# Graph convolution as (adjacency · features) · weight, SAGE weight sums moved into the feed-forward stage, and another order of sums in the SAGE layers

## The reference, cut to what matters

```
x = x + relu(diffusion(h))                                   # 3 hops over a symmetric adjacency
x = x + layernorm(x1 + gelu(x1 @ W_ffn1 + b) @ W_ffn2 + b2)  # x1: relational layer, 4 edge types
x = x + D^-1/2 (A + I) D^-1/2 @ (h @ weight) + bias          # graph convolution (GCN)
x = x + sage(relu(sage(h)))                                  # two SAGE layers:
#   sage(x) = mean over in-edges of x @ Wl.T + bl + x @ Wr.T
```

## Time and profile before

| what | us |
|---|---|
| median of three runs | 365.51 (364.59 to 366.06) |
| the profiled execution, its own time | 366.03 |
| span of that execution in the trace | 364.1 |
| PE busy | 346.9 (95%) |
| DVE, POOL, ACT busy | 245.3, 135.1, 83.8 |

### The profile page before, as it was taken

One profiled execution on the slowest core, in us unless ns is written; L12 is line 12 of the kernel. 1 busy time (PEld: TensorE's weight loads), 2 busy tenths in 40 slices (PEclk: granted clock), 3 DMA queues, 4 the chain that ended last, 5 costly groups with the idle time before them and its releaser, 6 DMA issues.

```text
span 364.1 us, 4411 instructions
## 1 busy us (share of the span) xinstructions
PE 346.9 (95%) x1633; PEld 243.7 (67%) x1633; DVE 245.3 (67%) x407; ACT 83.8 (23%) x183; POOL 135.1 (37%) x102
## 2 busy tenths in 40 slices
PE   8999999998999999999999999999998957999996
PEld 3459898773488888888888888444556423474444
DVE  5899999998798788913865220176896685354543
ACT  3556663314200000000010421213133401112110
POOL 5000000008799999997020200000880084522020
PEclk9999999999999999999999999999999896999999
DMA  7100005089100000512000986600510000000003
GB/s 249 40 2 3 2 2 225 8 198 367 70 0 2 1 0 2 189 43 72 17 2 4 275 201 107 108 0 0 90 28 1 1 0 0 2 2 0 0 0 117
DMA packets 43831, 22.08 MB, mean 61 GB/s; under 512 B 35552, under 2 KB 36064, under 8 KB 43808
## 3 DMA queue, kind: packets, MB, share of 16 engines
q1 hardware_dynamic: 43280, 20.85, 21.1%
q0 software_dynamic: 240, 0.79, 0.7%
q10 hardware_dynamic: 288, 0.13, 0.1%
HBM read 20.72 MB, written 1.05 MB: 60 GB/s over the span
## 4 chain that ended last, share of the span: by engine, by line
PE 79%; DVE 15%; ACT 2%; issue 2%; DMA 1%; ACTq 0%; DVEq 0%
PE bank L1463 14%; PE bank L1577 13%; PE bank L1520 13%; PE bank L1688 13%; PE bank L1643 6%; PE bank L604 4%; PE bank L1726 4%; PE bank L577 4%; PE bank L601 3%; PE bank L1451 2%; DVE h L1167 2%; PE bank L593 2%; DVE stats L1115 2%; DVE lo L1185 1%; DVE x L1131 1%
## 5 line engine op out<-in xcount | busy, mean ns | idle before, releaser
L995 ACT ACTIVATE columns<-mean_var,eps 128x1 f32<-128x1 f32 x20 | 5.9, 294 | 132.8 <-DVE mean_var L1116 132.8
L890 POOL TENSOR_TENSOR spare<-slots 128x512 f32<-128x512 f32 x4 | 6.0, 1491 | 76.0 <-PE bank L1463 75.3
L1577 PE MATMUL bank<-slots,wall 128*128 128x256 f32 x128 | 30.2, 380 | 0.0
L1463 PE MATMUL bank<-slots,h_t 128*128 128x512 f32 x64 | 28.7, 594 | 0.8 <-ACT h_t L1006 0.8
L1463 PE MATMUL bank<-h_t,spare 128*128 128x256 f32 x128 | 28.1, 379 | 0.0
L1643 PE MATMUL bank<-slots 128*128 128x512 f32 x64 | 27.8, 592 | 0.0
L604 PE MATMUL bank<-slots 128*128 128x112 bf16 x256 | 27.8, 228 | 0.0
L1688 PE MATMUL bank<-wall,h_t 128*128 128x512 f32 x48 | 24.1, 634 | 2.7 <-ACT h_t L1006 1.8
L1577 PEld LDWEIGHTS bank<-slots,wall 128*128 128x128 f32 x128 | 24.2, 190 | 3.2
L1463 PEld LDWEIGHTS bank<-h_t,spare 128*128 128x128 f32 x128 | 24.2, 190 | 3.2
L601 PE MATMUL bank<-slots 128*128 128x140 bf16 x128 | 26.2, 242 | 0.0
(11 more groups left out here) (248 smaller groups left out, 734.7 us busy)
## 6 DMA issues: line engine op xcount, KB each, us to landing
slots<-in_L_gnn_W_rel SPq DMA_DIRECT2D x4, 1024.0 KB, 10.7
spare<-in_L_gnn_W_ffn SPq DMA_DIRECT2D x1, 2048.0 KB, 8.0
slots<-in_L_gnn_W_ffn SPq DMA_DIRECT2D x1, 2048.0 KB, 8.6
slots<-in_L_gnn_Wl SPq DMA_DIRECT2D x32, 64.0 KB, 2.4
slots<-in_L_gnn_Wr SPq DMA_DIRECT2D x32, 64.0 KB, 2.5
x<-in_x SPq DMA_DIRECT2D x4, 256.0 KB, 5.9
bias<-in_L_gnn_W SPq DMA_DIRECT2D x2, 512.0 KB, 5.6
slots<-in_L_gnn_W_self SPq DMA_DIRECT2D x1, 1024.0 KB, 5.6
```

Source lines behind the costliest of these rows:

```text
L1463: ins = pe.matmul(bank, left, right, start=start and i == 0, stop=stop and i == len(pairs) - 1)
L1577: ins = pe.matmul(into, left[:, k, tile(p)], right[:, k, :], start=(n in (0, 2, 3, 5) and r == 0 and k == 0), stop=False, skip_group_check ...
```

## The change

- GCN: instead of `A · (h · weight)` the kernel computes `(A · scaled h) · weight`. ScalarE writes `hi = relu(...)` directly with the degree's root folded into the scale (`root_by_degree`), DVE makes the same value in fp32 (`h`) and the rest `lo`. `near(k, q, ...)` multiplies them by the adjacency with the features as output rows, so that its result, copied out of PSUM by ACT and DVE in turns, is already the left operand of the product with `w2`. The four fills of `h` for the GCN go.
- Adjacency: ACT thresholds the transposed counts with two RELUs (`adjacency`), POOL adds the identity.
- Loads and sums of the SAGE weights: SP starts `load_turned` 0, 1, 2, 3 in a row and then `w2`; DVE does all sixteen `turn` ahead of the down stage; POOL does `combine_own(0)` and `combine_own(1)` ahead of the four additions of `bf2`.
- SAGE: DVE does `sum_nodes(layer, 1)` behind P4's addition instead of ahead of P5's, `sum_nodes(0, 0)` earlier; PE makes the fills 0 and 1 of layer 0 inside the product with `w2`, and the fill of tile 2 stands behind P1.

```diff
-        w2 = place(0)
-        sage_raw = [place(1), place(2), place(3), place(4)]
+        w2 = spare[:, KT * N:2 * KT * N].rearrange("p (k n) -> p k n", k=KT)
+        sage_raw = [place(1), place(2), place(3), place(0)]
...
             load_turned(0, wl1_in)
-            sp.dma_start(w2, tiled(w2_in)).then_inc(w2_loaded, 16)
             load_turned(1, wr1_in)
             load_turned(2, wl2_in)
-            sp.wait_ge(down_ready, NT)
             load_turned(3, wr2_in)
+            sp.wait_ge(up_ready, GT)
+            sp.dma_start(w2, tiled(w2_in)).then_inc(w2_loaded, 16)
...
-            for t in FFN_TILES:
-                pool.wait_ge(t_ready, use_of(H_FFN, t) + 1)
-                pool.tensor_tensor(h[:, t, :], h[:, t, :], bf2, ALU.add).then_inc(ffn_biased, 1)
-            pool.wait_ge(late_rows_loaded, 16 * 3)
...
-            pool.wait_ge(down_ready, NT)
-            combine_own(0)
+            for layer in range(2):
+                combine_own(layer)
+            for t in FFN_TILES:
+                pool.wait_ge(t_ready, use_of(H_FFN, t) + 1)
+                pool.tensor_tensor(h[:, t, :], h[:, t, :], bf2, ALU.add).then_inc(ffn_biased, 1)
+            pool.wait_ge(late_rows_loaded, 16 * 3)
+
             for t in range(NT):
-                pool.wait_ge(h_ready[TO_GCN], t + 1)
+                own = adj[:, t, t * P:(t + 1) * P]
+                pool.wait_ge(steps_out, 2 * t + 2)
+                pool.tensor_tensor(own, own.bitcast(F32), ident[:], ALU.add).then_inc(adj_ready, 1)
+            for t in range(NT):
+                pool.wait_ge(gcn_lo, t + 1)
                 pool.tensor_tensor(x[:, t, :], x[:, t, :], b2, ALU.add).then_inc(gcn_biased, 1)
-            base(0, 0)
-            combine_own(1)
-            base(0, 1)
+            for p in range(2):
+                base(0, p)
...
+            def adjacency(t):
+
+                act.wait_ge(cnt_t_ready, t + 1)
+                act.activation(both_ways[:, t % 2, :], (misc_bank if t % 2 else cnt_bank)[:], ACT.Relu, bias=ones[:, 0:1], scale=-1.0)\
+                    .then_inc(steps_out, 1)
+                act.wait_ge(steps_out, 2 * t + 1)
+                act.activation(adj[:, t, :], both_ways[:, t % 2, :], ACT.Relu, bias=ones[:, 0:1], scale=-1.0).then_inc(steps_out, 1)
+
             for t in range(NT):
                 root(OUT_FFN, t)
-                root(TO_GCN, t)
-                norm_relu(TO_GCN, t)
+                if t == NT - 1:
+                    adjacency(3)
+                root_by_degree(t)
+                act.wait_ge(shift_ready[TO_GCN], t + 1)
+                act.activation(hi[1][:, t, :], x[:, t, :], ACT.Relu, bias=shift[:, t:t + 1], scale=rstd[:, t:t + 1])\
+                    .then_inc(gcn_hi, 1)
+                if t < NT - 1:
+                    adjacency(t)
...
-            for k in range(KT):
-                turn(0, k)
+            for q in range(4):
+                for k in range(KT):
+                    turn(q, k)
 
             for m in range(NT):
                 dve.wait_ge(down_ready, m + 1)
...
                 scale_and_shift(TO_GCN, m)
-                if m == 2:
-                    for k in range(KT):
-                        turn(1, k)
+                dve.wait_ge(shift_ready[TO_GCN], m + 1)
+                link(dve.tensor_scalar(h[:, m, :], x[:, m, :], rstd[:, m:m + 1], shift[:, m:m + 1], ALU.mult, ALU.add))
+                dve.wait_ge(gcn_hi, m + 1)
+                dve.scalar_tensor_tensor(lo[1][:, m, :], h[:, m, :], 0.0, hi[1][:, m, :].bitcast(F32), ALU.max, ALU.subtract)\
+                    .then_inc(gcn_lo, 1)
...
+                    dve.wait_ge(sage_ready[layer], made(p, P5))
+                    dve.wait_ge(based, 2 * done)
+                    dve.tensor_tensor(own[:, 2 * p + 1, :], p53[:], own[:, 2 * p + 1, :], ALU.add).then_inc(own_sum, 1)
+                    dve.wait_ge(sage_ready[layer], made(p, P4))
+                    dve.tensor_tensor(out_of_lower, p74[:], upper, ALU.add).then_inc(lower_out, 1)
                     if p == 0:
                         sum_nodes(layer, 1)
...
+            transpose_counts(range(2, NT))
+            for q in range(NT):
+                pe.wait_ge(adj_ready, NT + q + 1)
+                if q < NT - 1:
+                    pe.wait_ge(gcn_lo, q + 1)
+                    for k in range(KT):
+                        if q == 0:
+                            pe.wait_ge(down_out, k + 1)
+                        near(k, q, (hi, lo))
+                else:
+                    pe.wait_ge(gcn_hi, NT)
+                    for k in range(KT):
+                        near(k, q, (hi,))
+                    pe.wait_ge(gcn_lo, NT)
+                    for k in range(KT):
+                        near(k, q, (lo,))
             pe.wait_ge(w2_loaded, 16)
             for m in range(NT):
...
+                    if (m, k) in ((2, 2), (3, 2)):
+                        fill_h(H_SAGE1, m - 2, h_ready[TO_SAGE])
+                    ins = pe.matmul(gcn_bank[m][:], h_t[:, k, tile(m)], w2[:, k, :], start=(k == 0), stop=(k == KT - 1))
+                ins.then_inc(gcn_ready, 1)
```

More of the change, by code:

```diff
@@ L677, in build_matrices @@
     return tails, block_out
-H_REL, H_FFN, H_GCN, H_SAGE1, H_SAGE2 = range(5)
+H_REL, H_FFN, H_SAGE1, H_SAGE2 = range(4)
 FFN_TILES = [2, 0, 3, 1]
-FILLS = [(what, t) for what in (H_REL, H_FFN, H_GCN, H_SAGE1, H_SAGE2) for t in (FFN_TILES if what == H_FFN else range(NT))]
+FILLS = [(what, t) for what in (H_REL, H_FFN, H_SAGE1, H_SAGE2) for t in (FFN_TILES if what == H_FFN else range(NT))]
 B = 32
@@ L777, in run_blocks @@
         dw_inv = sb("dw_inv", [P, HOPS, NT], F32)
-        columns = sb("columns", [P, 8, NT], F32)
-        std, rstd, shift, row_sum, inv_row, out_deg, deg_root, inv_root = (columns[:, i, :] for i in range(8))
+        columns = sb("columns", [P, 9, NT], F32)
+        std, rstd, shift, row_sum, inv_row, out_deg, deg_root, inv_root, eps_deg = (columns[:, i, :] for i in range(9))
         in_degs, inv_degs = sb("in_degs", [P, 2 * NT], F32), sb("inv_degs", [P, 2 * NT], F32)
@@ L995, in root, with root_by_degree @@
                 act.activation(std[:, t:t + 1], mean_var[:, t, 1:2], ACT.Sqrt, bias=eps[:]).then_inc(std_ready[n], 1)
+            def root_by_degree(t):
+                act.wait_ge(var_ready[TO_GCN], t + 1)
+                act.activation(std[:, t:t + 1], mean_var[:, t, 1:2], ACT.Sqrt, bias=eps_deg[:, t:t + 1], scale=out_deg[:, t:t + 1])\
+                    .then_inc(std_ready[TO_GCN], 1)
             def norm_relu(n, t):
@@ L1408, in _ @@
                 own = (h, x)[layer]
-                sum_nodes(layer, 0)
+                if layer == 1:
+                    sum_nodes(layer, 0)
                 for p in range(2):
@@ L1418, in _ @@
                     dve.wait_ge(first_kept, done)
-                    dve.tensor_tensor(upper, p6[:], first, ALU.add).then_inc(upper_sum, 1)
+                    dve.tensor_tensor(upper, p6[:], first, ALU.add).then_inc(sage_sum, 1)
                     if p == 1:
@@ L1647, in _, with near @@
-            transpose_counts(range(2))
+            def near(k, q, parts):
+                ins = product(main[k][:], [(part[1][:, q, tile(k)], adj[:, q, :]) for part in parts],
+                              start=(q == 0 and hi in parts), stop=(q == NT - 1 and lo in parts))
+                if q == NT - 1 and lo in parts:
+                    ins.then_inc(near_ready, 1)
+            transpose_counts(range(2, NT))
[14 more added lines that the diff above has]
+                        near(k, q, (lo,))
@@ L1696, in sage_products @@
                 for n in SAGE_ORDER[p]:
+                    if (layer, p) == (0, 0) and n in (P6, P7, P5):
+                        pe.wait_ge(gcn_out, 2 + (P6, P7, P5).index(n))
                     if n == P2:
@@ L1723, in mean @@
                         pe.wait_ge(out_lo, NT * layer + q + 1)
-                    for part in (hi[1 - layer], lo[1 - layer]):
+                    for part in (hi[layer], lo[layer]):
                         left, right = (cnt_r, part[:, q, :]) if exact else (wall[:, R], part[:, q, :].bitcast(F32))
-                        ins = pe.matmul(main[m][:], left[:, q, tile(m)], right, start=(q == 0 and part is hi[1 - layer]),
-                                        stop=(q == NT - 1 and part is lo[1 - layer]))
+                        ins = pe.matmul(main[m][:], left[:, q, tile(m)], right, start=(q == 0 and part is hi[layer]),
+                                        stop=(q == NT - 1 and part is lo[layer]))
                 ins.then_inc(mean_ready[layer], 1)
```

175 lines of the change are left out of this document (68 added, 107 removed).

## The result

| | median us | range | beside it: before |
|---|---|---|---|
| changed kernel, 4 runs | 374.59 | 374.13 to 376.56 | 365.78 (364.59 to 366.73) |

The ratio is 1.0248, with a 95% interval of [1.0205, 1.0291]: 8.8 us slower, where the prediction had 373.0 us and 90% for slower.

What follows compares the result with a forecast made beforehand. PE was taken to bound the kernel, busy 346.9 of 364.1 us. SAGE, 11.7 us shorter at 69.9, would start at 301.7 behind the delayed queues: span 371.6, 373.0 us in terms of the runs, range 369.5 to 379.5.

Steps and rivals of the forecast that it cites:

- 2: weight 3 turned: DVE's queue: four turns take 2.49 us after the last load lands at 240.5, so weight 3 is turned at 243.0.
- no hole at P3: PE in SAGE layer 0: the hole of 6.67 us goes, 6.84 us off.
- Step 1: SP's queue: loads 1 to 3 take 8.5 us each, are issued by 238.6, and the last lands at 240.5.
- Step 3: POOL's queue: combine_own(1) starts at 243.0, takes 9.9 us and is over at 252.9.
- Step 4: Down stage: DVE's first addition waits for two bf2 additions of 1.26 us each, starting at 255.5 instead of 234.4.
- only one queue counts: Down stage, rival: bf2 additions not held behind the combinations, DVE starts 12.5 us earlier, time 360.5; chance 6% for faster.
- The chain of the four tiles: DVE and ACT behind the down product: four tiles in sequence, 7.2 us each, 28.8 in all.
- Contention on tile 3: DVE's last chain beside POOL's GCN bias additions: between 0 and 2.5 us, middle 1.3 taken.
- The clock: PE at half clock after idling, around the product with w2: 0.5 us added, bounds 0 and 1.8.
- SAGE: From the first SAGE product to the end: 11.7 us off 81.64, so 69.9 us.
- first half-clock term: PE at the first SAGE product, 282.46: half clock behind the hole goes, 3.57 - 1.72 = 1.85 us off.

Runs made afterwards that it cites:

- Experiment 1: The changed kernel with POOL's additions of bf2 moved ahead of both combinations of SAGE weights: 366.01 us, ratio to before 1.0014.
- Experiment 6: The changed kernel with POOL's four additions of the GCN bias all behind the last lo: 373.32 us, ratio to before 1.0246.
- experiments 3, 4 and 5: The kernel before with combine_own(1) behind base(0, 1), 357.74 us; with sum_nodes(layer, 1) behind the additions for P5 and P4, 358.81 us; with both edits, 356.31 us.

## Why the prediction was right

Its numbers beside those of the changed kernel, 2.3 taken off for the late start:

| step | predicted | measured | off |
|---|---|---|---|
| 1: last load issued | 238.6 | 240.1 | +1.5 |
| 2: weight 3 turned | 243.0 | 244.3 | +1.3 |
| 3: `combine_own(1)` done | 252.9 | 253.8 | +0.9 |
| 4: first down addition | 255.5 | 256.3 | +0.8 |
| last `lo` ready | 285.6 | 286.4 | +0.8 |
| product with `w2` starts | 286.6 | 287.8 | +1.2 |
| first SAGE product | 301.7 | 302.5 | +0.8 |
| end of the span | 371.6 | 372.4 | +0.8 |

What was to show it, shows: the first addition released by L973, and 43.5 us of idleness on DVE up to it, broken only by turns; 18.0 us of idle PE, where more than 10 were foretold; no hole at P3; SAGE 70 us long. Point by point:

- **Step 1 was mis-sized by 1.5 us**, the largest error. With `w2` out of the way load 1 still took 9.80 us, between the 8.5 taken and the 12.00 of before; so about 2.2 of the excess were `w2`'s doing and 1.3 were not. The other traces agree: this load took 9.18 to 9.88 us in the five experiments with `w2` behind the loads, 11.64 to 12.40 in the three with `w2` in front of it. What the 1.3 are was not tried.
- **Step 3 came out 0.4 shorter**, which took back part of that: four instructions of 2.34 to 2.35 us. The shortest of the earlier trace rows were the right price for POOL alone.
- **Step 4 held, and so did its cause.** Experiment 1 removed just this wait and took 8.6 us off. The rival "only one queue counts" had this as its way to faster, with a price of 12.5 us: the wait was indeed 12.05 long, but 3.9 came back as contention, so even with it the kernel would not have been faster. That price had left the contention out.
- **The chain of the four tiles** took 7.18 us a tile for 7.2.
- **Contention on tile 3** was 1.3, the middle that was taken. Both operations were held, the fp32 copy of `h` (0.55 to 1.23) as well as `lo` (0.69 to 1.67), though neither for a whole POOL instruction. Here the rule of the Trainium skill that the prediction weighed ("SBUF — State Buffer", "Who interferes with whom") told what the first rows couldn't: that a tensor_scalar of 128x512 loses time too. It is not true of every tensor_scalar: one of 128x1 at 285.54, beside the same additions, took its usual 0.21 us. Experiment 6 gives the 1.3 back on DVE, though not at the end of the kernel.
- **The clock** cost 0 of the 0.5 taken. The windows of the changed kernel (length, busy us of PE, PEld, DVE, ACT, POOL with their counts; then the granted clock, DMA share, GB/s) show half clock from 264 on:

```profile
264.00:272.00 8.00, 1.11 (x4) 0.71 (x4) 6.39 (x14) 3.35 (x6) 0.46 (x1) 0.50 0.00 0
272.00:280.00 8.00, 3.68 (x10) 2.57 (x10) 6.10 (x13) 3.61 (x7) 0.45 (x1) 0.50 0.00 0
280.00:284.00 4.00, 3.12 (x7) 2.51 (x8) 3.40 (x8) 2.31 (x4) 0.95 (x2) 0.50 0.01 2
284.00:288.00 4.00, 4.00 (x14) 3.18 (x13) 3.41 (x6) 1.20 (x2) 4.00 (x4) 0.73 0.00 0
288.00:292.00 4.00, 3.82 (x12) 1.88 (x12) 2.00 (x3) 1.08 (x2) 1.47 (x2) 1.00 0.01 4
```

  All of it lies over adjacency products that wait for DVE anyhow. PE was back at full clock at 286, before the product with `w2` began. The reason given for hiding it was right, but it held by little: the products ahead of `lo` were through at about 288.5 (287.58 and four of 0.23), and `lo` was ready at 288.72. The prediction had them done long beforehand. Experiment 6, with `lo` earlier, paid for the half clock. 0.3 of the 0.5 went into the hand-over from `lo` instead, 1.3 us for 1.0.
- **SAGE** lasted 69.95 us for 69.9. That sum was right in total, but experiments 3, 4 and 5 show that its first half-clock term (1.85 us at 282.46) was not bound to the wait in front of it: the same wait was followed by full clock in all three. In the changed kernel the wait is gone too, so against the profiled execution the term came out right. Against most runs of before it is too large: the mean granted clock of the profiled execution was 0.986, that of 22 of the 24 later runs of before 0.991, and the stretch of the earlier trace rows at 282.40 makes just this difference ((1 - 0.60) x 4.30 / 364.1 = 0.005). So, by this estimate, most runs of before never had that half clock to lose.

The median is 1.6 above the forecast. 0.8 of that is in the table. The rest, 0.8, is how an execution's span stands to the median: the forecast added 1.4 to its span, and here it is 374.59 - 372.4 = 2.2. In each run the time is about 1.9 above its own span; the 0.5 that the forecast took off again was the distance of before's profiled execution to its median. That this distance comes from the half clock at 282.46 fits the granted clocks, but was not shown. The mechanism held at every step; that the sum came out within 0.8 us owes something to luck, since the errors of steps 1 and 3 had opposite signs and the half clock was covered by 0.2 us.

## What to carry to other kernels

Work that is pulled forward in an in-order queue is not free because its engine idles there: ask which instruction now stands behind its wait, and when the data it waits for lands. Here two such queues cost 20 us while the gain they were part of was 12, and most of that gain was to be had by moving one call over another. A combination on GpSimd belongs where VectorE reads PSUM or small columns, since beside operations with two SBUF inputs it costs the latter up to a whole instruction each.

## What was not expected of the hardware

- The same wait of 1.82 to 1.83 us ahead of the first SAGE product was followed by half clock once (3.57 us for four records, 0.60 granted) and by full clock three times (1.95 to 1.96, experiments 3 to 5). A short wait does not settle by itself what the clock does.
- In the changed kernel the granted clock stayed at 0.50, the 1.2 GHz level, from 264 to 284, over idle pieces and pieces of work alike, and rose in the window from 284 to 288, when PE had been at work without a pause since 280.88. The Trainium skill ("TensorE: Matmul & The Clock Gate", "What's actually happening") has the half level as the default that activity lifts; the windows agree.
- POOL pays for the shared use as well: an addition of 128x1024 takes 2.34 to 2.35 us alone and up to 2.80 beside DVE in experiment 1. The timeline of POOL there:

```profile
244.56 2.35 POOL L953 TENSOR_TENSOR slots<-wall 128x1024 f32<-128x1024 f32 x1 [7.41 <-DVE wall L1359]
...
249.63 2.80 POOL L956 TENSOR_TENSOR wall<-wall 128x1024 f32<-128x1024 f32 x1
```
